# A two-layer graph kernel on one core: node features loaded already transposed, first on SyncE's queue, small constants as one load, skip features loaded later

## The reference, cut to what matters

```python
def _L0_gnn_ref(x, adj, W1, b1, W2, b2):
    A = adj + jnp.eye(n)
    deg = A.sum(axis=1)
    d = jnp.where(deg > 0, jax.lax.rsqrt(deg), 0.0)
    An = d[:, None] * A * d[None, :]
    h = jax.nn.relu(An @ (x @ W1) + b1)
    return An @ (h @ W2) + b2

x = _layernorm(x + _L0_gnn_ref(x, adj, ...))      # x here is the skip
x = _layernorm(x + _L1_gnn_ref(x, adj, ff0_w, ff1_w, attn_w, ...))
```

## Time and profile before

| | us |
|---|---|
| median of 3 runs (1073.17 to 1074.48) | 1073.35 |
| the profiled execution, its own time | 1074.81 |
| span of its trace | 1073.0 |
| TensorE busy in the span | 987.0 (92%) |
| DMA in the chain that ended last | 11% of the span |
| ScalarE's DMA issues in that chain (L473 and L488) | 2% of the span |

### The profile page before, as it was taken

One profiled execution on the slowest core, in us unless ns is written; L12 is line 12 of the kernel. 1 busy time (PEld: TensorE's weight loads), 2 busy tenths in 40 slices (PEclk: granted clock), 3 DMA queues, 4 the chain that ended last, 5 costly groups with the idle time before them and its releaser, 6 DMA issues.

```text
span 1073.0 us, 9333 instructions
## 1 busy us (share of the span) xinstructions
PE 987.0 (92%) x2622; PEld 480.3 (45%) x2624; DVE 698.7 (65%) x1250; ACT 504.0 (47%) x731; POOL 110.8 (10%) x144
## 2 busy tenths in 40 slices
PE   5498899999999999999869999999999999999980
PEld 5243344444644444444554444444444444444440
DVE  0467666655265344443828767788889999988873
ACT  3443332221100000000257765978696888888753
POOL 4011111111000000000610000101010001010111
PEclk9699999999999999999869999999999999999995
DMA  8899999999365999996023132222223232323201
GB/s 299 340 428 427 429 425 426 425 423 375 133 264 225 374 385 379 376 393 262 1 60 99 59 98 69 70 88 71 96 69 89 89 98 89 98 89 99 82 8 39
DMA packets 66666, 223.93 MB, mean 209 GB/s; under 512 B 5248, under 2 KB 49856, under 8 KB 56640
## 3 DMA queue, kind: packets, MB, share of 16 engines
q1 hardware_dynamic: 55600, 203.90, 49.9%
q10 hardware_dynamic: 11024, 19.57, 4.8%
HBM read 203.49 MB, written 19.96 MB: 208 GB/s over the span
## 4 chain that ended last, share of the span: by engine, by line
PE 75%; DMA 11%; ACT 5%; POOL 2%; issue 2%; ACTq 2%; DVE 2%; POOLq 0%; DVEq 0%
PE ps L1110 75%; DMA W<-in_adj 11%; ACT W L493 3%; ACTq L488 1%; POOL rstd L425 1%; ACTq L473 1%; POOL r L432 1%; ACT T L573 1%; ACT final L619 1%; DVE T L884 0%; ACT mix L602 0%; ACT squares L593 0%; POOL rs L443 0%; PE ps L1142 0%; POOL r L431 0%
## 5 line engine op out<-in xcount | busy, mean ns | idle before, releaser
L1110 PE MATMUL ps<-colbuf,stat 128*128 128x512 f32 x992 | 437.5, 597 | 29.4 <-DVE diag L726 28.8
L1110 PE MATMUL ps<-T,Yw 128*128 128x512 f32 x1024 | 445.6, 595 | 9.6 <-DVE T L884 9.6
L884 DVE SCALAR_TENSOR_TENSOR T<-T,mring 128x2048 f32<-128x2048 f32 x128 | 292.8, 2289 | 67.2 <-ACT T L573 66.7
L573 ACT ACTIVATE T<-Rrow,small,ratio 128x1024 f32<-128x1024 f32 x256 | 301.3, 1230 | 70.9 <-PE ps L1110 70.6
L1110 PEld LDWEIGHTS ps<-T,Yw 128*128 128x128 f32 x1024 | 195.4, 191 | 246.1 <-issue 230.8
L1110 PEld LDWEIGHTS ps<-colbuf,stat 128*128 128x128 f32 x992 | 186.1, 191 | 250.4 <-issue 218.2
L493 ACT ACTIVATE W<-W 128x4096 f32<-128x4096 f32 (+30 forms) x32 | 66.1, 2066 | 146.5 <-DMA W<-in_adj 136.6
L512 ACT ACTIVATE stat<-xw_g 128x128 f32 (+1 forms) x32 | 9.9, 310 | 197.8 <-PE ps L1110 170.1
L765 DVE TENSOR_SCALAR mtile<-colbuf 128x4096 uint8<-128x4096 f32 x30 | 69.0, 2300 | 17.8 <-DMA mask<-mtile 15.9
L761 DVE TENSOR_TENSOR colbuf<-colbuf,ident 128x128 f32 (+1 forms) x26 | 7.6, 292 | 90.2 <-DMA colbuf<-in_adjT 90.1
L686 DVE TENSOR_TENSOR W<-W,colbuf 128x3712 f32<-128x3712 f32 (+28 forms) x29 | 62.3, 2149 | 0.0
(11 more groups left out here) (152 smaller groups left out, 614.9 us busy)
## 6 DMA issues: line engine op xcount, KB each, us to landing
colbuf<-in_adjT SPq DMA_DIRECT2D x58, 2048.0 KB, 12.2
mring<-mask SPq DMA_DIRECT2D x128, 256.0 KB, 2.7
mask<-mtile ACTq DMA_DIRECT2D x32, 512.0 KB, 10.2
Rrow<-s_src SPq DMA_DIRECT2D x9, 512.0 KB, 4.4
W<-in_adj SPq DMA_DIRECT2D x2, 2048.0 KB, 12.8
W<-in_adjT SPq DMA_DIRECT2D x2, 2048.0 KB, 12.9
out<-final SPq DMA_DIRECT2D x6, 512.0 KB, 3.9
W<-in_x ACTq DMA_DIRECT2D x8, 256.0 KB, 6.1
```

What stands on the lines that cost most here:

```text
L573: last = act.activation(T[:, c % TS, j, :], Rrow[:, g % 2, :], ACT.Relu, scale=ratio[:, c * JB + j:c * JB + j + 1], bias=small[:, 8:9])
L884: v.scalar_tensor_tensor(out=tile, in0=tile, scalar=1.0, in1=mring[:, c % TS, :, :].rearrange("p b n -> p (b n)"), op0=ALU.add, op1=ALU.mu ...
L1110: return pe.matmul(*args, skip_group_check=True, **kw)
```

## The change

- xT (x transposed by the host) is an input. SyncE loads it first of all, in eight slices of 256 KB, straight to xT0. TensorE's transposes and ScalarE's copies of them are gone.
- SyncE no longer waits for x before the adjacency loads. They stand directly behind xT on its queue.
- W2, the ff0, ff1 and attention weights and the four vectors are joined by the host to one array of 128 x 904 f32, and loaded by one DMA that SyncE issues behind the transposed block 4.
- x for the skip is laid out by the host so that each partition reads one piece of 16 KB. SyncE loads it in one DMA behind the two early loads between the aggregations; GpSimd's eight additions stand behind its reductions of the weight products.
- ScalarE does one square root of a constant at the start. One wait for "all first loads" becomes one for W1 and one for the biases.

```diff
@@ SyncE
-            sp.wait_ge(x_loaded[NG // 2], 16)
+            for k in range(NG):
+                sp.dma_start(xT0[:, cols(k, GW)], t["xT"][:, cols(k, GW)]).then_inc(x_loaded[k], 16)
             for b in range(B):
...
                 sp.dma_start(colbuf[:, u, :], adj_cols[b, :, :]).then_inc(col_loaded[u], 16)
+                if b == RING:
+                    sp.dma_start(weights[:, 0:t["weights"].shape[1]], t["weights"]).then_inc(consts, 16)
...
                 sp.dma_start(rowbuf[:, u, :], dram_block(adj_cols, u)).then_inc(row_loaded[u], 16)
+            sp.dma_start(x1, t["x"]).then_inc(skip_loaded, 16)
@@ GpSimd
-            pool.wait_ge(first_loaded, ALL_FIRST)
-            for k in range(NG):
-                pool.wait_ge(xT_done, k + 1)
-                pool.tensor_tensor(x1[:, group(k), :], x1[:, group(k), :],
-                                   b2bc[:, :].unsqueeze(1).broadcast_to([P, BPG, C]), ALU.add).then_inc(skip_ready, 1)
...
+            pool.wait_ge(biases_loaded, ALL_BIASES)
+            pool.wait_ge(skip_loaded, 16)
+            for k in range(NG):
+                pool.tensor_tensor(x1[:, group(k), :], x1[:, group(k), :],
+                                   b2bc[:, :].unsqueeze(1).broadcast_to([P, BPG, C]), ALU.add).then_inc(skip_ready, 1)
@@ ScalarE
-            for dst, src in FIRST:
-                act.dma_start(dst, src).then_inc(first_loaded, 16)
-            for k in range(NG):
-                act.dma_start(x1[:, group(k), :], t["x"].rearrange("(b p) c -> p b c", p=P)[:, group(k), :])\
-                    .then_inc(x_loaded[k], 16)
+            act.dma_start(w1[:, :], t["W1"]).then_inc(first_loaded, 16)
+            for dst, src in BIASES:
+                act.dma_start(dst, src).then_inc(biases_loaded, 16)
+            act.wait_ge(zeros_ready, 3)
+            act.activation(small[:, 10:11], small[:, 9:10], ACT.Sqrt)
...
-            for i in range(NG + 1):
-                k = i
-                if k < NG:
-                    act.wait_ge(xT_done, k + 1)
-                    act.activation(xT0[:, cols(k, GW)], ps[:, k, :], ACT.Copy).then_inc(xT_ready, 1)
-                k = i - 1
-                if k >= 0:
-                    act.wait_ge(xw_done, k + 1)
-                    act.activation(xw_g[:, group(k), :].rearrange("p b c -> p (b c)"), ps[:, k, :], ACT.Copy)\
-                        .then_inc(xw_ready, 1)
-            for dst, src in CONSTS:
-                act.dma_start(dst, src).then_inc(consts, 16)
+            for k in range(NG):
+                act.wait_ge(xw_done, k + 1)
+                act.activation(xw_g[:, group(k), :].rearrange("p b c -> p (b c)"), ps[:, k, :], ACT.Copy).then_inc(xw_ready, 1)
@@ TensorE
-            pe.wait_ge(first_loaded, ALL_FIRST)
+            pe.wait_ge(first_loaded, 16)
+            for k in range(NG):
+                pe.wait_ge(x_loaded[k], 16)
+                for b in range(k * BPG, (k + 1) * BPG):
+                    last = multiply(ps[:, k, cols(b % BPG)], xT0[:, cols(b)], w1[:, :], start=True, stop=True)
+                last.then_inc(xw_done, 1)
+            pe.wait_ge(biases_loaded, ALL_BIASES)
             pe.wait_ge(ident_ready, 4)
```

More of the change, by code:

```diff
@@ L65, in build @@
 def build(nc, t, out):
-    N, C = t["x"].shape
-    K = t["ff0"].shape[0]
+    N, C = t["adj"].shape[0], t["W1"].shape[0]
+    K = (t["weights"].shape[1] - C - 4) // (3 * C + 2)
     B = N // P
@@ L92, in build @@
         W = sb("W", [P, 4, B, C], F32)
+        weights = sb("weights", [P, t["weights"].shape[1] + 1], F32)
+        KC = K * C
+        w2 = weights[:, 0:C]
+        ff0, ff0T, ff1T = (weights[:, C + m * KC:C + (m + 1) * KC].rearrange("p (k c) -> p k c", c=C) for m in range(3))
+        attnT = weights[:, C + 3 * KC:C + 3 * KC + 2 * K].rearrange("p (k s) -> p k s", s=2)
+        vec = weights[:, C + 3 * KC + 2 * K:C + 3 * KC + 2 * K + 5]
         Z0, X1, Z1, ACC = range(4)
@@ L165, in build @@
         w1 = sb("w1", [P, C], F32, first)
-        w2 = sb("w2", [P, C], F32, first)
         b1bc = sb("b1bc", [P, C], F32, first)
         b2bc = sb("b2bc", [P, C], F32, first)
-        ff0 = sb("ff0", [P, K, C], F32, first)
-        ff0T = sb("ff0T", [P, K, C], F32, first)
         gain_mix = sb("gain_mix", [P, P], F32, first)
@@ L190, in build @@
         x_loaded = [sem(f"x_loaded{k}") for k in range(NG)]
-        first_loaded, consts, xT_done, xT_ready, ident_ready, zeros_ready, skip_ready = sems(
-            "first_loaded consts xT_done xT_ready ident_ready zeros_ready skip_ready")
+        first_loaded, consts, biases_loaded, skip_loaded, ident_ready, zeros_ready, skip_ready = sems(
+            "first_loaded consts biases_loaded skip_loaded ident_ready zeros_ready skip_ready")
         row_loaded = sems("row_loaded0 row_loaded1")
@@ L246, in cols @@
             return slice(k * n, (k + 1) * n)
[L248 to L259, removed]
+        BIASES = [(b1bc[:, :], t["b1"].partition_broadcast(P)), (b2bc[:, :], t["b2"].partition_broadcast(P))]
+        ALL_BIASES = 16 * len(BIASES)
         ROW_CREDIT, COL_CREDIT = 2, RING
@@ L674, in _ @@
             v.memset(small[:, 8:9], -1.0).then_inc(zeros_ready, 1)
+            v.memset(small[:, 9:10], 1.0).then_inc(zeros_ready, 1)
             v.wait_ge(ident_ready, 4)
@@ L727, in _ @@
             v.tensor_tensor(d2_all[:, :], d_all[:, :], d_all[:, :], ALU.mult).then_inc(mix_step, 1)
-            v.wait_ge(consts, ALL_CONSTS)
+            v.wait_ge(consts, 16)
             v.tensor_tensor(vec[:, 4:5], vec[:, 1:2], vec[:, 0:1], ALU.subtract).then_inc(mix_step, 1)
@@ L1134, in _ @@
             pe.sem_inc(chunk_done, TS)
-            pe.wait_ge(first_loaded, ALL_FIRST)
-            pe.wait_ge(ident_ready, 4)
[L1137 to L1149, removed]
-            pe.wait_ge(zeros_ready, 2)
+            pe.wait_ge(first_loaded, 16)
[5 more added lines that the diff above has]
+            pe.wait_ge(biases_loaded, ALL_BIASES)
+            pe.wait_ge(ident_ready, 4)
+            pe.wait_ge(zeros_ready, 3)
             for k in range(NG):
@@ L1167, in _ @@
             add_bias(ps[:, NG - 1, cols(u)], u)
-            pe.wait_ge(consts, ALL_CONSTS)
+            pe.wait_ge(consts, 16)
             for i in range(NG + SN):
@@ L1309, in _ @@
                 ending(s, last_phase, 1)
-_INS = ["x", "adj", "adjT", "W1", "b1", "W2", "b2", "ff0", "ff0T", "ff1T", "attnT",
-        "ln1_g", "ln1_b", "ln2_g", "ln2_b"]
+_INS = ["x", "xT", "adj", "adjT", "W1", "b1", "b2", "weights"]
 def kernel(x, adj, L0_gnn_W1, L0_gnn_b1, L0_gnn_W2, L0_gnn_b2, L1_gnn_ff0_w, L1_gnn_ff1_w, L1_gnn_attn_w,
@@ L1323 @@
     heads, c = ff0.shape[0], ff0.shape[1]
+    x = np.asarray(x)
+    parts = [np.asarray(L0_gnn_W2), ff0.transpose(1, 0, 2), ff0.transpose(2, 0, 1), ff1.transpose(2, 0, 1),
+             attn.reshape(heads, 2, c).transpose(2, 0, 1), *(np.asarray(v) for v in (L1_gnn_g1, L1_gnn_b1, L1_gnn_g2, L1_gnn_b2))]
     given = {
-        "x": x, "adj": adj, "adjT": np.asarray(adj).T,
-        "W1": L0_gnn_W1, "b1": L0_gnn_b1, "W2": L0_gnn_W2, "b2": L0_gnn_b2,
-        "ff0": ff0, "ff0T": ff0.transpose(0, 2, 1), "ff1T": ff1.transpose(0, 2, 1),
-        "attnT": attn.reshape(heads, 2, c).transpose(2, 0, 1),
-        "ln1_g": L1_gnn_g1, "ln1_b": L1_gnn_b1, "ln2_g": L1_gnn_g2, "ln2_b": L1_gnn_b2,
+        "x": x.reshape(-1, P, c).transpose(1, 0, 2), "xT": x.T, "adj": adj, "adjT": np.asarray(adj).T,
+        "W1": L0_gnn_W1, "b1": L0_gnn_b1, "b2": L0_gnn_b2,
+        "weights": np.concatenate([part.reshape(c, -1) for part in parts], axis=1),
     }
@@ L1333 @@
     t = {name: nc.dram_tensor(f"in_{name}", arrays[name].shape, F32, kind="ExternalInput").ap() for name in _INS}
-    out = nc.dram_tensor("out", arrays["x"].shape, F32, kind="ExternalOutput").ap()
+    out = nc.dram_tensor("out", x.shape, F32, kind="ExternalOutput").ap()
     build(nc, t, out)
```

3 lines of the change are left out of this document (removed).

## The result

The changed kernel takes 1065.1 us (median of 4 runs, 1063.90 to 1065.98) beside 1073.91 us of the kernel before in the same comparison: ratio 0.9915, 95% interval 0.9903 to 0.9927. A second comparison on another occasion gave 0.9919 (0.9905 to 0.9932). The mean of the two, 0.9917, is 8.9 us. Forecast were 10.8 us and 1062.6, in a range of 1059.8 to 1066.0. The direction is right and the time lies in the range, but the gain is 1.9 us smaller than forecast. The forecast's own terms reached only to 1063.5; 1065.1 lies nearer to the rival of a slow xT (1066.0).

The account below looks back on a forecast made before the run. Loads bound the kernel up to block 18, then TensorE. Row block 2 landing 11.8 us earlier, less 1.1 for constants, plus 0.1 of slack, gave 10.8 us: from 1073.35 to 1062.6 us, range 1059.8 to 1066.0.

Parts of the forecast that it names:

- the rival of a slow xT: Start of SyncE's queue: xT at 243 GB/s delays the adjacency behind it; lead 7.4 us, 1066.0 us; chance 0.07.
- What bounds the kernel: First aggregation: loads set the pace from 60 to 188 us at 427 GB/s; from 188.14 us TensorE does.
- The hinge at block 18: First aggregation: an earlier landing of row block 18 moves block 18 and all that follows; lead 10.8 us.
- The constants on ScalarE: Start: nine constant issues held row sum 0 until 34.23 us; moved into the load stream, they cost 1.08 us.
- xT's own rate: First load: xT's 2 KB pieces, 16 KB apart, run at 399 GB/s, taking 5.25 instead of 4.91 us, +0.34.
- My other end: Slow bound for xT's load: 243 GB/s at a share of one, from x's 512-byte pieces; 8.63 us, +3.7.
- Latency and spread, 2.95 us: Start: time a load into an empty queue takes beyond its transfer, added to the landing of row block 2.
- TensorE's own line, 27 us in hand: First aggregation: TensorE alone could reach block 18 at 150 us; the loads let it start at 177.3.
- The rival's mechanism: Early blocks: waiting TensorE's clock stays at 1.2 GHz, about 7.1 us more per block; eight give 1092; chance 0.03.
- a clock of 0.50 past block 1: Sign in the changed profile that the prediction is wrong: TensorE's clock still reading 0.50 after block 1.
- its price without cover: Load of x for the skip falling in the second aggregation: 4.9 us lost, 1067.5 us; uncovered-work rival's chance 0.04.
- GpSimd's additions: Start of second aggregation: eight additions, 10.1 us, beside VectorE's first masks; VectorE's extra between 0 and 10.1, taken as 0.

Follow-up runs that it names:

- the added load: Changed kernel with one more 2.10 MB load of x between xT and the first adjacency block: 1069.50 us, ratio 0.9959 to the kernel before.
- the experiment: Changed kernel with the load of x for the skip behind the first four reloads of the second aggregation, not ahead: 1064.86 us, ratio 0.9920 to the kernel before.

## Why the prediction was right, and where it was off

- **What bounds the kernel: right. The hinge at block 18: right for that trace only.** That the loads set the pace until TensorE has no gap left is shown by the added load: 4.72 us at row sum 2, 4.72 at row sum 18, 4.73 at the end of the second aggregation. But the block where this happens isn't fixed. The chain of the changed kernel leaves the loads at block 15 and not at 18, and TensorE's last idle time stands before block 14 (0.24 us). The kernel before was there too: its blocks 15, 16 and 17 had no idle time, and the 0.60 us before block 18 came from a single delay of its rows. At block 15 the lead is 8.44 us, at block 18 9.20:

```profile
165.73 7.13 PE L1110 MATMUL ps<-colbuf,stat 128*128 128x512 f32 x16
```

  So 0.8 us of the 9.2 exist because the kernel before lost them between these blocks.
- **The constants on ScalarE: right.** Alone they give 4.6 us. Their place in the stream costs 1.12 us, forecast 1.08.
- **xT's own rate: the term that was mis-sized.** The prediction took 399 GB/s from row block 29, because it had the same form, and +0.34 us. Measured were 185 and 192 GB/s between 4 and 8 us, below even the 243 that the prediction held to be the other end (315 to 324 with the biases away, between the two ends), and row sum 0 began 2.6 us and row sum 2 3.87 us later than forecast. The other traces divide the 3.87 roughly: about 1.3 us is a single delay at row block 2 (37.71, and 36.40 with contiguous slices; the kernel with later constants, the same up to there, has 36.32), 0.85 the biases (36.40 and 35.55), and 1.4 the pieces and loads of small size (35.55 and 34.15, whose constants come later but behind row block 2). What remains is 0.3. At row sum 3 the same steps are 1.1 for the biases (46.69 and 45.61) and 0.7 for the pieces and loads (45.61 and 44.95); equal kernels differ there by up to 0.9. So the biases and the small pieces together cost about 2 us, and how it divides between them is not known to better than about 1 us. The row that I chose ran as a small part between transposed blocks in 16 KB pieces, so that its stretch showed mostly the rate of those. My other end, x in small pieces at 292 GB/s and a share of 1.20, was nearer, and I had kept it as a rival with 0.07 (1066.0).
- **Latency and spread, 2.95 us: about right.** With large pieces and the biases away, row sum 2 began 0.3 us after the 33.84 in which this term stands. What it consists of, no view divides.
- **Why 8.9 and not 6.9.** With row sum 2 only 7.96 us early, the lead should have been 6.9 at the hinge. It was 9.41, because the kernel before had single delays at row sums 4, 11 and 18 (about 0.5, 0.95 and 0.9 us, read as an interval that is longer than its neighbours, such as 9.25 where 8.3 was due) and the changed kernel between 5 and 18 none. The prediction had one such delay in its range, and none in its sum. That the gain is 1.9 us and not 3.9 us below the forecast is therefore luck: delays of about 2.4 us in the kernel before hid that much of the xT term, and the prediction had not counted on them.
- **TensorE's own line, 27 us in hand: right, and needed.** The rival's mechanism did appear. Stretches of the changed kernel:

```profile
46.00:48.00 2.00, 0.14 (x1) 0.14 (x1) 1.86 (x8) 0.96 (x1) 0.99 (x1) 0.50 1.00 426
50.00:56.00 6.00, 6.00 (x12) 2.53 (x12) 5.20 (x8) 0.74 (x3) 1.01 (x1) 0.78 1.00 423
```

  After a wait of 5.52 us before block 2 the granted clock was at 1.2 GHz again, and the block took 9.47 us. Block 5, after 2.71 us of waiting, took 8.83 us, with the clock at 0.62 and 0.52 in the two stretches from 76 to 80 us. The prediction had named a clock of 0.50 past block 1 as a sign of being wrong; it came, and the slack took it.
- **x for the skip: covered, as said; its price without cover was wrong.** It landed at 274.9 us, 20 us before the first reload. I put 4.9 us on a load without cover, and the experiment shows none.
- **GpSimd's additions: covered, but not free on VectorE as I took.** From the timeline of the changed kernel:

```profile
297.09 12.42 POOL L405 TENSOR_TENSOR W<-W,b2bc 128x512 f32<-128x512 f32 x8 [6.92 <-issue]
297.77 1.23 DVE L754 TENSOR_TENSOR mtile<-mtile,ident_u 128x128 uint8<-128x128 uint8 x1
...
305.39 2.99 DVE L751 TENSOR_SCALAR mtile<-colbuf 128x4096 uint8<-128x4096 f32 x1 [6.38 <-DMA mask<-mtile]
308.42 1.24 DVE L754 TENSOR_TENSOR mtile<-mtile,ident_u 128x128 uint8<-128x128 uint8 x1
```

  The additions took 12.42 instead of 10.1 us, two of VectorE's small operations 1.23 and 1.24 instead of 0.29, a mask 2.99 instead of 2.29. That is 2.6 us more on VectorE, between my bounds of 0 and 10.1, and all of it lay in the slack before block 4. The additions also began at 297.09 and not near 288.6; the 6.92 us before them are put down to "issue", and no run explains them.
- **The distance between the pieces: no cost at 16 KB.** With pieces 2 KB and 16 KB apart, row sum 0 began at 16.97 and 16.90 us, so the 2.6 us that it came late have another cause. The Trainium skill, "DMA: Bandwidth & Descriptors", section "Latency and other measured facts", has copies between HBM tensors at 103 GB/s in each direction with rows 4 MiB apart, and at 214 once 4 KiB are added to that distance; the smallest distance in its list is 512 KiB, with 207. No run here has rows so far apart.

What stays open: the single delays of about 0.9 us. They don't look random. The one at row sum 11 is missing in all six traces that load xT in eight slices beside the biases and without the wait, and in the one with the constants alone moved (8.26 to 8.29 us for that interval), and stands in the other five and in the kernel before (8.78 to 9.25). In the trace of before, each interval of row landings with such a delay, and few of the others, holds one packet of an instruction queue. But in the changed kernel such packets also fall between row sums 3 and 4 and between 9 and 11, and in the kernel with contiguous slices between 1 and 2, without a delay. Whether instruction loading causes them isn't settled; I have not found a way to move it alone. Also open is the 1.7 us by which the two spans differ further in the attention layer; the medians don't show it.

## What to carry to other kernels

An engine that both issues loads and computes is a queue: nine small issues held the sum that lets the next load go for 9.9 us here, and cost 4.6 us of the kernel's time. Find the block at which the pace passes from the loads to the compute engine; bytes put ahead of it cost their full time, bytes behind it nothing. For the first loads of a program, take large pieces per partition in few loads, and keep one-row broadcasts out of their way. A lead of 1 us read at one place of one trace can be a single delay that fell elsewhere: compare several places and a second trace.

## What the runs showed of the hardware

- Between 4 and 8 us, loads of 256 KB in pieces of 2 KB moved 315 to 324 GB/s at DMA shares of 1.01 to 1.03 (biases away), and one load in pieces of 16 KB 414 to 464 GB/s at shares of 0.98 to 1.10. A full share doesn't show the loss.
- With two broadcasts of 512 bytes to 128 partitions, 0.13 MB together, beside the eight slices of xT, the share of the DMA engines was 0.54 to 0.89 from 4 to 8 us in seven traces; with the broadcasts moved away it was 1.01 and 1.03.
- While GpSimd's additions with two f32 inputs ran, VectorE's 128x128 byte operation took 1.23 and 1.24 us, and 0.29 before and after.
- TensorE's clock was at 1.2 GHz (granted clock 0.50 and 0.52) after waits of 5.52 us and of 2.71 us, and stayed at 2.4 GHz through a wait of 2.21 us.
